# A feed-forward that narrows straight into rows, with the residual rows made by Pool, and a reordered first stage, in a graph attention layer

## The reference

```python
h = jnp.maximum(_layernorm(x), 0.0)
hs = where(smask, layer_norm(h, ln1_scale, ln1_bias), 0)      # source rows
ht = where(tmask, layer_norm(h_target, ln1_scale, ln1_bias), 0)
q = (ht @ Wq + bq) / sqrt(32); k = hs @ Wk + bk; v = hs @ Wv + bv
probs = softmax(where(adj != 0, q @ k.T, -1e30))              # per head
ht = ht + where(tmask, (probs @ v) @ Wo + bo, 0)
ht = where(tmask, layer_norm(ht, ln2_scale, ln2_bias), 0)
ff = gelu(ht @ W1) @ W2                                       # 256 -> 1024 -> 256
out = x + ht + ff
```

## Time and profile before

| | us |
|---|---|
| median of 3 runs | 491.09 |
| lowest, highest | 490.02, 492.01 |
| profiled execution, its own time | 489.83 |
| its span in the trace | 488.1 |
| TensorE busy | 472.1 (97%) |
| DVE busy | 418.4 (86%) |
| ScalarE busy | 376.5 (77%) |
| Pool busy | 305.6 (63%) |

### The profile page before, as it was taken

One profiled execution on the slowest core, in us unless ns is written; L12 is line 12 of the kernel. 1 busy time (PEld: TensorE's weight loads), 2 busy tenths in 40 slices (PEclk: granted clock), 3 DMA queues, 4 the chain that ended last, 5 costly groups with the idle time before them and its releaser, 6 DMA issues.

```text
span 488.1 us, 10628 instructions
## 1 busy us (share of the span) xinstructions
PE 472.1 (97%) x4366; PEld 243.2 (50%) x4366; DVE 418.4 (86%) x631; ACT 376.5 (77%) x462; POOL 305.6 (63%) x152
## 2 busy tenths in 40 slices
PE   3999989999999999999999999999999999999995
PEld 1557533343333333343333333343435888888884
DVE  6889499999999999999999999999997977566243
ACT  4887979998998998998998998999995571727150
POOL 1000019977998999999999998999998300000000
PEclk9999999999999999999999999999999999999999
DMA  8997879925432673232763400500000100202021
GB/s 231 243 217 133 157 216 385 346 47 109 172 69 47 76 173 58 44 52 50 77 177 57 77 2 3 186 35 1 2 2 1 46 33 13 87 1 86 1 87 45
DMA packets 53775, 46.93 MB, mean 96 GB/s; under 512 B 35486, under 2 KB 46652, under 8 KB 53212
## 3 DMA queue, kind: packets, MB, share of 16 engines
q1 hardware_dynamic: 51216, 37.30, 28.7%
q0 software_dynamic: 2480, 8.92, 10.4%
q10 hardware_dynamic: 28, 0.01, 0.0%
HBM read 31.93 MB, written 14.81 MB: 96 GB/s over the span
## 4 chain that ended last, share of the span: by engine, by line
PE 72%; DVE 11%; issue 9%; ACT 4%; POOL 3%; DMA 1%; DVEq 0%; POOLq 0%
PE acc L1434 18%; PE slot L1419 16%; PE acc L1452 8%; DVE probs L1044 8%; PE slot L1536 3%; PE slot L1534 3%; PE slot L1535 3%; PE slot L1322 3%; PE acc L1571 2%; PE acc L1573 2%; PE acc L1572 2%; PE slot L1485 2%; POOL added_up L554 2%; DVE stats L865 1%; PE slot L1342 1%
## 5 line engine op out<-in xcount | busy, mean ns | idle before, releaser
L1044 DVE SCALAR_TENSOR_TENSOR probs<-maskT,slot 128x1024 f32<-128x1024 uint16 x256 | 298.0, 1217 | 6.1 <-PE slot L1419 5.7
L759 ACT ACTIVATE probs<-probs 128x1024 f32<-128x1024 f32 x256 | 266.8, 1057 | 22.3 <-DVE probs L1044 4.8
L554 POOL TENSOR_TENSOR added_up<-added_up,probs 128x1024 f32<-128x1024 f32 x96 | 226.8, 2411 | 0.2
L1434 PE MATMUL acc<-probs,V 128*32 128x512 f32 x1024 | 136.3, 604 | 1.8 <-DVE q_lo_staged L970 1.8
L1452 PE MATMUL acc<-probs,ones 128*32 128x256 f32 x1024 | 77.0, 379 | 0.0
L1452 PEld LDWEIGHTS acc<-probs,ones 128*32 128x32 f32 x1024 | 33.3, 110 | 72.8 <-issue 71.2
L1419 PE MATMUL slot<-q_hi,k_hi 32*128 32x512 f32 x512 | 64.4, 493 | 0.9 <-DVE probs L1044 0.3
L823 ACT ACTIVATE g_full<-slot 128x512 f32<-128x512 f32 x32 | 19.3, 602 | 45.2 <-issue 30.0
L1419 PEld LDWEIGHTS slot<-q_hi,k_hi 32*128 32x128 f32 x512 | 24.5, 181 | 59.1 <-DVE probs L1044 54.4
L551 POOL TENSOR_TENSOR added_up<-probs 128x1024 f32<-128x1024 f32 x16 | 38.1, 2406 | 24.9 <-ACT probs L759 15.0
L1419 PE MATMUL slot<-q_lo,k_hi 32*128 32x512 f32 x512 | 51.8, 391 | 0.0
(11 more groups left out here) (144 smaller groups left out, 496.6 us busy)
## 6 DMA issues: line engine op xcount, KB each, us to landing
adj_raw<-in_adj POOLq DMA_DIRECT2D x16, 512.0 KB, 5.5
htn<-in_L_gnn_h_target SPq DMA_DIRECT2D x4, 512.0 KB, 7.4
ht_saved<-htn SPq DMA_DIRECT2D x1, 2048.0 KB, 8.1
k_hi_saved<-k_hi SPq DMA_DIRECT2D x1, 2048.0 KB, 10.2
k_lo_saved<-k_lo SPq DMA_DIRECT2D x1, 2048.0 KB, 14.5
v_saved<-V SPq DMA_DIRECT2D x1, 2048.0 KB, 8.9
inverse<-inverse_saved SPq DMA_DIRECT2D x8, 256.0 KB
maskT<-in_L_gnn_W SPq DMA_DIRECT2D x2, 1024.0 KB, 6.4
```

The costliest lines, as they stand in the source:

```text
L554: nc.gpsimd.tensor_tensor(added_up[:, pair], added_up[:, pair], at(i), ALU.add).then_inc(added, 1)
L759: nc.scalar.activation(p, p, ACT.Exp).then_inc(exped, 1)
L1044: nc.vector.scalar_tensor_tensor(out=probs[:, u % RING], in0=m, scalar=-HALF_EDGE, in1=slot[u % SLOTS][:], op0=ALU.add, op1=ALU.min).then_ ...
L1434: mm = pe.matmul(acc[HD * j:HD * j + HD, 0, :], V[:, i, h * HD:(h + 1) * HD], probs[:, (PAIRS * k + j // 2) % RING, j % 2, :], start=(i == 0),
```

## The change

Narrowing. The stationary operand is now a block of `g_hi` or `g_lo` (128 features by 128 rows) and W2 moves: 8 blocks f x 4 tiles t x 3 matmuls of 256 columns, and the result stands in rows. `turn_out`, `join`, `out_T`, `narrow_last` and `finish_last` are gone. In the last chunk each tile has a PSUM bank of its own, and the last two blocks f are done tile by tile, so that each tile's row is finished, and stored, while the next is narrowed.

What the rows are added to. Since the shifted and scaled y is now wanted in rows too, Pool makes it in place in `htn`: y times ln2_scale, plus ln2_bias, times the node mask, plus the x rows (`make_rows`, four instructions a chunk). Two new row vectors are loaded for it. DVE's `finish` adds `htn` in place of `xr`, after the split of block 4 in place of 1. The flag's transposition moves from behind the last `widen` to its head.

First stage. `wo` is loaded before the x rows of chunk 2; the test of the node row is in two parts, the first ahead of `half_scale`; `mask_beta(0)` stands before the first normalising and the others behind `rectify_chunk`; the bias product stands ahead of keys(0) in place of a warm-up product; `centre` of the next chunk goes ahead of `keys_lo`; statistics wait tile by tile; and the inverse root takes the node mask in without a step of its own.

```diff
@@ SP: loads, stores
             sp.dma_start(wk[:], Wk.rearrange("(c p) n -> p c n", p=P)).then_inc(wk_in, 16)
+            sp.dma_start(wo[:], Wo.rearrange("(c p) n -> p c n", p=P)).then_inc(wo_in, 16)
             sp.dma_start(xs[:, rows_of(2), :], x_rows[:, rows_of(2), :]).then_inc(x_in[2], 16)
...
-            sp.dma_start(wo[:], Wo.rearrange("(c p) n -> p c n", p=P)).then_inc(wo_in, 16)
...
+            for dst, src in ((gamma2_row[:], ln2_scale), (beta2_row[:], ln2_bias)):
+                sp.dma_start(dst, row_vector(src)).then_inc(rows2_in, 16)
             for c in range(LAST):
+                sp.wait_ge(rows_made, 4 * (c + 1))
+                sp.dma_start(xr[:], x_rows[:, rows_of(c + 1), :]).then_inc(x_again, 16)
...
+            for t in range(TILES):
+                sp.wait_ge(summed, TILES * LAST + t + 1)
+                sp.dma_start(out_rows[:, LAST * TILES + t, :], result[:, t, :]).then_inc(stored, 16)
@@ Pool
+            def make_rows(c):
+                h = htn[:, rows_of(c), :]
+                pool.wait_ge(y_turned, c + 1)
+                if c == 0:
+                    pool.wait_ge(rows2_in, 16 * 2)
+                if c + 2 < NCH:
+                    pool.wait_ge(norm_y, LN2 * (c + 3))
+                nc.gpsimd.tensor_tensor(h, h, gamma2_row[:, None, :].to_broadcast(wide), ALU.mult
+                                        ).then_inc(rows_made, 1)
...
+                nc.gpsimd.tensor_tensor(h, h, beta2_row[:, None, :].to_broadcast(wide), ALU.add
...
+                nc.gpsimd.tensor_tensor(h, h, nodes[:, rows_of(c)][:, :, None].to_broadcast(wide), ALU.mult
...
+                pool.wait_ge(x_again, 16 * (c + 1))
+                nc.gpsimd.tensor_tensor(h, h, xr[:], ALU.add).then_inc(rows_made, 1)
+            for c in range(NCH):
+                make_rows(c)
@@ ScalarE
+            mask_beta(0)
             normalise_half(0)
             normalise_half(1)
-            mask_beta(0)
...
+            rectify_chunk(2)
             mask_beta(2)
-            rectify_chunk(2)
@@ DVE
             def finish(c):
-                dve.wait_ge(x_again, 16 * (c + 1))
+                dve.wait_ge(rows_made, 4 * (c + 1))
...
-                    elif c and f == 1:
+                    elif c == LAST and f == 1:
+                        make_flag()
+                    elif c and f == 4:
                         finish(c - 1)
@@ TensorE
-            warm_up(2)
+            warm_up(1)
+            project_rest()
             keys(0)
...
             def narrow(c):
+                alone = c == LAST
...
+                tail = FC - 2 if c == LAST else FC
+                order = [(f, t) for f in range(tail) for t in range(TILES)]
+                order += [(f, t) for t in range(TILES) for f in range(tail, FC)]
+                for f, t in order:
+                    ts, dst = slice(t * P, (t + 1) * P), narrow_place(c, t)
+                    if t == 0:
+                        pe.wait_ge(gelu_lo, c * FC + f + 1)
+                    pe.matmul(dst, g_hi[:, f, ts], w2_hi[:, f, :], start=(f == 0 and (alone or t % 2 == 0)), stop=False)
+                    pe.matmul(dst, g_hi[:, f, ts], w2_lo[:, f, :], start=False, stop=False)
+                    mm = pe.matmul(dst, g_lo[:, f, ts], w2_hi[:, f, :], start=False, stop=(f == FC - 1 and (alone or t % 2 == 1)))
+                    if f == FC - 1:
+                        mm.then_inc(narrowed, 1)
```

More of the change, by code:

```diff
@@ L484, in _ @@
                     general = load_flag(sp, "sp")
[L485 to L489, removed]
+            for t in range(TILES):
+                sp.wait_ge(summed, TILES * LAST + t + 1)
+                sp.dma_start(out_rows[:, LAST * TILES + t, :], result[:, t, :]).then_inc(stored, 16)
+            sp.wait_ge(stored, 32 * LAST + 16 * TILES)
             with sp.If(general):
@@ L706, in _ @@
             root_half(1)
+            mask_beta(0)
             normalise_half(0)
             normalise_half(1)
-            mask_beta(0)
+            act.wait_ge(made, 3)
+            for d in range(DC):
+                nc.scalar.activation(bv_wide[:, d, :], ident[:], ACT.Identity, bias=bv_col[:, d:d + 1], scale=0.0
+                                     ).then_inc(bv_spread, 1)
             rectify_chunk(1)
@@ L862, in _, with row_stats @@
         def _(dve):
-            def row_stats(src, t0, into, into0, signal, done, tiles=TILES):
+            def row_stats(src, t0, into, into0, signal, done, tiles=TILES, ready=None):
                 for t in range(tiles):
+                    if ready is not None:
+                        dve.wait_ge(ready, t0 + t + 1)
                     nc.vector.bn_stats(stats[:, t, :], src[:, t0 + t, :]).then_inc(signal, 1)
@@ L869, in row_stats, with inverse_root @@
                 dve.wait_ge(signal, done + 2 * tiles)
-            def inverse_root(w, r, signal, done, tiles=TILES):
+            def inverse_root(w, r, signal, done, tiles=TILES, wanted=None):
                 step = newton[:, 0:tiles, :]
@@ L876, in inverse_root @@
                 nc.vector.tensor_tensor(step, r, r, ALU.mult).then_inc(signal, 1)
+                if wanted is not None:
+                    nc.vector.tensor_tensor(r, r, wanted, ALU.mult).then_inc(signal, 1)
+                    done += 1
                 dve.wait_ge(signal, done + 2)
@@ L991, in _ @@
             half_scale(1)
-            test_nodes()
             centre(1)
             source_affine(0)
+            test_nodes(slice(CHUNK, S))
             source_stats(1)
             source_scale(1)
+            centre(2)
             keys_lo(0)
-            centre(2)
             source_affine(1)
@@ L1203, in _ @@
                     find_largest()
-                else:
-                    make_flag()
-                if c < LAST:
-                    join(c)
                 if c == 0:
                     add_residual(LAST)
-            finish_last()
+            finish(LAST)
             general = load_flag(dve, "dve")
```

142 lines of the change are left out of this document (35 added, 107 removed).

## The result

| | before | changed kernel |
|---|---|---|
| median | 490.64 (6 runs) | 498.05 (6 runs) |
| lowest, highest | 490.02, 492.01 | 496.72, 501.33 |
| profiled execution, its own time | 489.83 | 497.03 |
| its span | 488.1 | 495.0 |
| granted clock of TensorE | 0.998 | 0.991 |

The ratio is 1.0146, 95% interval 1.0125 to 1.0167: slower by 7.2 us in the profiled executions and 7.4 in the medians.

What follows compares the result with a forecast made beforehand. TensorE was taken to bound the kernel, full until the last slice. Terms -2.7 - 2.2 + 1.4 + 8.9 + 0 gave +5.4 us, on a median of 491.1: 496.5, own range 493.6 to 500.6, stated range 488.5 to 501.0.

Steps and rivals of the forecast that it cites:

- transposes, end, pace together: Network stage: output transposes removed -2.7, shorter last chunk's end -2.2, narrowing in 256-column matmuls +1.4; -3.5 us in all.
- wait before narrowing 1: TensorE waits 2.0 us for finish(0), as chunk 1's splits stand still behind make_rows(0) on Pool.
- wait before narrowing 2: TensorE waits 5.4 us for finish(1), as chunk 2's splits are held by the rows for chunks 1 and 2.
- wait before widening 3: Widening 3 starts 1.5 us late: the flag's transposition at its head waits for find_largest, behind held DVE subtractions.
- first stage: Late node row delays keys(0), but the stage gains later and keys(3) start where they did: zero, ends -1.9 and +1.5.
- Pool against DVE: Network stage: DVE splits meeting make_rows wait for a Pool instruction's end, and TensorE behind them; +8.9 us, the largest term.
- Pace of narrowing: Narrowing's 96 matmuls of 256 columns a chunk take 0.117 us each, between 0.113 and 0.120: 1.4 us lost.
- the one without a hold-up: Rival: make_rows is hidden and splits wait less than about 0.6 us on average; -3.5, 487.6, faster; chance 0.16.
- Costly matmuls: Rival: in narrowing, 256 columns cost what 512 do; some 35 us more, 525; chance 0.04.
- holding in one direction only: Rival: Pool is not held by DVE; waits are 5.7, sum +2.2 to +2.5, 493.5; chance 0.10.

Runs made afterwards that it cites:

- The pieces: The changed kernel with each of its 16 Pool instructions of 128x1024 cut in four of 128x256: 493.68, ratio 1.0056 of before.

## Why the prediction was right, and where its sizes were off

It said 496.5, slower, and 498.05 was measured, inside the forecast's own range. The forecast stood on a median of 491.1 for the kernel before, and six runs of it give 490.64; so the change was put at +5.4 and came to +7.4. By its steps, against the network stage of one execution:

| term | predicted | measured |
|---|---|---|
| transposes, end, pace together | -2.7 - 2.2 + 1.4 = -3.5 | -2.26 |
| wait before narrowing 1 | 2.0 | 2.26 |
| wait before narrowing 2 | 5.4 | 5.18 |
| wait before widening 3 | 1.5 | 0 |
| clock | not foreseen | 2.0 |
| first stage | 0 | 0 |
| sum | +5.4 | +7.2 |

The two waits count from where the first matmul would have started behind the transposes (423.81 and 449.38, by the 0.79 it takes in the kernel with Pool's work left out) to where it did, 426.07 and 454.56. The clock's 2.0 is narrowing 2 with nothing else in it, 454.56 to 468.16, 13.60, less the 11.60 of that same kernel.

- **Pool against DVE**, the term that decided, was right in mechanism and size: 7.4 for the two waits that it put at 7.4. That the sums agree to 0.1 is luck, since the first wait came 0.26 longer and the second 0.22 shorter. It rested on a single row, the 1.57 us split of the earlier trace rows. The layout by queue gave `finish(0)` its end at 425.8 and `finish(1)` at 454.2; they came at 426.0 and 454.5. Pool is held too, by 0.27 to 0.45 an instruction. The prediction's reason for taking 2.7 between its starts (the whole rest of the split, less a first part of Pool's instruction that goes on all the same) is borne out: the split of 444.50 ends at 447.39, 0.59 after Pool's start at 446.80, and Pool loses 0.44. The first part is some 0.13 to 0.20 us by these rows, where 0.22 was taken. The distance of starts from 446.80 on is 2.67 in the mean, but it is 2.30 behind the instruction with the mask column, which is shorter and which the prediction had put at 2.40 too, and 2.66 to 2.93 behind the others. The Trainium skill (SBUF — State Buffer, "Who interferes with whom") says that whichever of the two issues first has the pair of SBUF ports that they share for its whole instruction. The trace agrees in both directions, but for that first part, and for the second of two splits in a row, which went ahead of a Pool instruction already begun (449.64, above). The same section of the Trainium skill also says that tensor_scalar can contend and that a DVE instruction with at most one SBUF input doesn't outside such modes, and the rows of both kinds above agree.
- **Pace of narrowing** was mis-sized: the step "no row decides between the two, so I take 0.117". Matmuls of 256 columns start 0.12 us apart, the fixed-overhead end. Where nothing interferes narrowing 2 takes 11.60 us (448.84 to 460.44), not 10.9: 0.7 a chunk, 2.8 in place of 1.4. With it the first line becomes -2.1, close to the -2.26. Between two ends, one of which needed 512 columns to have no fixed part at all, the other was the one to take.
- **The clock** was missing. The prediction said that each wait put before TensorE "costs its whole length", and counted nothing more; this one also left TensorE at 1.2 GHz for 4.5 us of the work behind it.
- **Widening 3** didn't wait, since the slow clock ended narrowing 2 at 468.16, after the reduction (466.5). With the clock kept up the wait appeared, 0.85 and 0.35. So the wait that the step foresaw exists, but at 0.35 to 0.85 and not 1.5.
- **First stage**: zero for the median was right, for an incomplete reason. The node row landed at 9.98 and keys(3) came 0.4 earlier in that execution, while three of nine, those with the fall in the first stage, reached the network 1.6 to 3.3 us later than before did (379.15 to 380.84 against 377.59); two more came 0.8 and 1.5 later. The prediction knew that source rows would be 1.5 to 2 us late and asked only what queue that delays, not what an idle TensorE does.

The pace (+1.4), the clock (+2.0) and the absent wait (-1.5) are 1.9 together, against the 2.0 by which the medians' difference exceeds the forecast's. So a hit inside the range owes something to errors of opposite sign.

Of the rivals, the one without a hold-up is refuted: its 487.6 is what the kernel gives when Pool's work is left out (488.03, 2.65 under before where -3.5 was forecast), so it priced the rest fairly well. Costly matmuls are refuted by the 0.12; holding in one direction only is refuted by Pool's 2.67 to 2.85.

## What to carry to other kernels

Work given to an idle Pool is not free when DVE works on SBUF at the same time: each DVE instruction that meets it can stand still to the end of Pool's instruction, and with it every engine behind DVE. Make Pool's instructions few, put them where DVE waits or works from PSUM, or cut them short; here count and place together were worth 9 us of the network stage. And price a wait of TensorE at its length plus the slow clock that may follow it.

## What the runs showed of the hardware

- TensorE's clock fell to 0.50 after waits of 4.94, 4.95, 2.87 and 2.22 us in the network and after 2.08, 1.95 and 1.44 in the first stage; after waits of 2.04, 2.00, 1.79, 1.24 and 1.21 it stayed at 1.00. So the length of one wait doesn't decide alone. The one profile of the kernel before, without such waits, shows no fall in either place. In the first stage two matmuls of the warm-up then took 1.91 in place of 1.02; they did so too in one execution after a wait of 0.68, where the listed clock is 1.00.
- DVE and Pool, each with two operands in SBUF, keep each other out. A split ends 0.54 to 0.56 after the Pool instruction that held it. Pool loses what is left of the split when it starts (0.46 to 1.06 us), less 0.13 to 0.20.
- Pool's 128x1024 took 2.40 with two full operands. With a column as one it took 2.22 in all four cases of the changed kernel, but each of them started while a held split was still running. The pieces show that such an instruction is held as well: 0.61 for 128x256 where DVE makes no such subtraction, and up to 1.14 where it does.

```profile
446.96 3.64 POOL L627 TENSOR_TENSOR htn<-htn,nodes 128x256 f32<-128x256 f32 x4
...
462.16 2.33 POOL L627 TENSOR_TENSOR htn<-htn,nodes 128x256 f32<-128x256 f32 x4
```

- The network's 256-column matmuls with new weights each start 0.12 us apart, 512-column ones 0.227: about 0.013 us a matmul that doesn't shrink with the columns.
